# Weight remainders one item later on VectorE, and the last visit's down products tile by tile

## The reference

```python
x = layernorm(x + attention(x))            # 16 heads of 16 features
x = layernorm(x + recurrence(x, ctx))      # a scan over the tokens with exp(k), exp(-k)
x = layernorm(x + moe(x))

def moe(x):                                # E=8 experts, K=128 tokens for each: every token
    Sm = swapaxes(softmax(x @ Wg.T), 1, 2)
    G, I = top_k(Sm, K)
    ex = take_along_axis(x[:, None], I[..., None], axis=2)
    h1 = gelu(ex @ W1 + b1)                # 256 -> 1024
    out = G[..., None] * (h1 @ W2 + b2)    # 1024 -> 256
    return zeros_like(x).at[arange(b), I].add(out)
```

## Time and profile before

| | us |
|---|---|
| runs, median (lowest, highest) | 942.67 (942.16, 943.93) |
| the profiled execution, its time | 944.04 |
| its span | 942.3 |
| TensorE busy | 892.0 |
| VectorE busy | 599.3 |
| ScalarE busy | 579.7 |
| GpSimd busy | 79.2 |

### The profile page before, as it was taken

The page is one execution under the profiler, slowest core; times in us unless marked ns, Lnnn a source line. Parts: engine busy times, 40 slices in busy tenths (PEclk is TensorE's granted clock), DMA queues, the critical chain, the costliest instruction groups (busy, mean ns, idle before and its releaser), DMA issues.

```text
span 942.3 us, 17858 instructions
## 1 busy us (share of the span) xinstructions
PE 892.0 (95%) x6672; PEld 815.4 (87%) x6672; DVE 599.3 (64%) x1246; ACT 579.7 (62%) x991; POOL 79.2 (8%) x116
## 2 busy tenths in 40 slices
PE   4759888999999999999999999999999999999997
PEld 3659888889988988989998989889998999899997
DVE  5888879777656574665676564656756564433574
ACT  4438875786655666665566666655666665444684
POOL 2330012000110010200120001200110000000000
PEclk8669989999999999999999999999999999999999
DMA  7617999967755554555645454554545455555340
GB/s 226 211 48 247 363 349 314 316 211 247 234 179 151 172 163 144 165 169 156 187 127 177 159 183 153 151 175 156 173 131 184 148 173 167 191 192 164 114 137 12
DMA packets 144693, 172.43 MB, mean 183 GB/s; under 512 B 11208, under 2 KB 110816, under 8 KB 144608
## 3 DMA queue, kind: packets, MB, share of 16 engines
q1 hardware_dynamic: 144608, 171.29, 56.6%
HBM read 135.60 MB, written 35.65 MB: 182 GB/s over the span
## 4 chain that ended last, share of the span: by engine, by line
PE 85%; DVE 8%; ACT 4%; issue 1%; DMA 0%; POOL 0%; SPq 0%; POOLq 0%; ACTq 0%; DVEq 0%
PE down_ps L736 13%; PE down_ps L737 12%; PE down_ps L738 12%; PE up_ps L511 12%; PE up_ps L513 12%; PE up_ps L512 12%; PE bank L564 2%; PE bank L511 2%; PE bank L513 1%; PE bank L512 1%; PE bank L550 1%; PE bank L533 1%; DVE w_lo L893 1%; ACT h_all L836 1%; PE bank L582 1%
## 5 line engine op out<-in xcount | busy, mean ns | idle before, releaser
L836 ACT ACTIVATE h_all<-up_ps,b_all 128x512 f32<-128x512 f32 (+1 forms) x296 | 183.3, 635 | 256.7 <-PE up_ps L513 255.2
L893 DVE TENSOR_TENSOR h_lo<-h_all,h_hi 128x512 fp32r<-128x512 f32 x256 | 177.5, 693 | 221.3 <-ACT h_hi L827 220.8
L736 PE MATMUL down_ps<-w_hi,h_hi 128*128 128x256 f32 x1024 | 295.3, 288 | 2.9 <-DVE acc L1074 2.9
L737 PE MATMUL down_ps<-w_lo,h_hi 128*128 128x256 f32 x1024 | 289.9, 283 | 0.0
L738 PE MATMUL down_ps<-w_hi,h_lo 128*128 128x256 f32 x1024 | 289.6, 283 | 0.0
L511 PE MATMUL up_ps<-x2t_hi,w_hi 128*128 128x512 f32 (+1 forms) x592 | 222.5, 376 | 1.6 <-DVE x2t_lo L893 0.9
L513 PE MATMUL up_ps<-x2t_hi,w_lo 128*128 128x512 f32 (+1 forms) x592 | 217.1, 367 | 0.0
L512 PE MATMUL up_ps<-x2t_lo,w_hi 128*128 128x512 f32 (+1 forms) x592 | 216.3, 365 | 0.0
L736 PEld LDWEIGHTS down_ps<-w_hi,h_hi 128*128 128x128 f32 x1024 | 195.3, 191 | 11.6 <-issue 2.0
L737 PEld LDWEIGHTS down_ps<-w_lo,h_hi 128*128 128x128 f32 x1024 | 196.0, 191 | 6.8
L738 PEld LDWEIGHTS down_ps<-w_hi,h_lo 128*128 128x128 f32 x1024 | 195.8, 191 | 0.0
(11 more groups left out here) (193 smaller groups left out, 997.7 us busy)
## 6 DMA issues: line engine op xcount, KB each, us to landing
w_hi<-w_parts SPq DMA_DIRECT2D x200, 256.0 KB, 3.0
w_lo<-w_parts SPq DMA_DIRECT2D x200, 256.0 KB, 3.3
w_raw<-in_w_dram SPq DMA_DIRECT2D x96, 256.0 KB, 4.0
w_parts<-w_hi SPq DMA_DIRECT2D x64, 256.0 KB, 3.9
w_parts<-w_lo SPq DMA_DIRECT2D x64, 256.0 KB, 4.3
x_in<-in_x_dram SPq DMA_DIRECT2D x8, 256.0 KB, 3.8
ctx_sb<-in_ctx_dram SPq DMA_DIRECT2D x8, 256.0 KB, 3.9
out_dram<-acc SPq DMA_DIRECT2D x8, 256.0 KB, 2.5
```

The lines of the kernel that those rows point to most:

```text
L736: nc.tensor.matmul(ps, hi, w2h[:, c, :], start=c == 0 and j == 0, stop=False, skip_group_check=True)
L737: nc.tensor.matmul(ps, hi, w2l[:, c, :], start=False, stop=False, skip_group_check=True)
L836: a = nc.scalar.activation(h_all[:, unit % HALL, k * wide:(k + 1) * wide], up_ps[unit % 2][:, k * wide:(k + 1) * wide], ACT.Gelu_apprx_tan ...
L893: return nc.vector.tensor_tensor(dst, src, hi.bitcast(F32), ALU.subtract)
```

## The change

First, VectorE takes the remainder of a weight piece with the item behind the one on which ScalarE rounds it (`splits_before`). Within an item the remainder stays the last but one thing it does. ScalarE and SyncE keep their places in the line. Second, the four down steps of the last visit are replaced by `last_down(0)` and `last_down(1)`: the products of tile 0 for all four units, then those of tile 1, each tile in a bank of its own. Each tile then has its own sum, statistics, root, norm and store of 128 KB.

```diff
+    def splits_before(i):
+
+        return [piece for n in range(VISITS) for k in range(len(ITEMS[n])) if FIRST_ITEM[n] + k == i - 1 for piece in splits(n, k)]
...
-            store(NPAIR - 1)
-            sp.wait_ge(stored, 16 * NPAIR)
+            for t in range(PAIR):
+                sp.wait_ge(out_ready, NPAIR + t)
+                sp.dma_start(out[PAIR * (NPAIR - 1) + t], acc[:, (NPAIR - 1) % 2, t]).then_inc(stored, 16)
+            sp.wait_ge(stored, 16 * (NPAIR + 1))
...
+            def last_down(j):
+
+                n = VISITS - 1
+                free = [freed(n, 0), EVACUATED[n]][j]
+                pe.wait_ge(added, free)
+                for u in range(G):
+                    weights(n, 1, u)
+                    pe.wait_ge(h_ready, FIRST_UNIT[n] + u + 1)
+                    for k in range(2):
+                        c = 2 * u + k
+                        cols = slice(k * TOK + j * S, k * TOK + (j + 1) * S)
+                        ps = by_tile(down_ps[(down_banks(n)[0] + j) % 2])[:, j, :]
+                        slot = (FIRST_UNIT[n] + u) % HALF
+                        mm = product(ps, h_hi[:, slot, cols], h_lo[:, slot, cols], w2h[:, c, :], w2l[:, c, :], c == 0, c == FC - 1)
+                mm.then_inc(last_done, 1)
...
-                    else:
+                    elif visit < VISITS - 1:
                         down(visit, u)
...
+            for j in range(PAIR):
+                last_down(j)
...
+            def finish_last(t):
+
+                n, p = VISITS - 1, NPAIR - 1
+                tile = acc[:, p % 2, t]
+                dve.wait_ge(last_done, t + 1)
+                nc.vector.scalar_tensor_tensor(out=tile, in0=by_tile(down_ps[(down_banks(n)[0] + t) % 2])[:, t, :],
+                                               scalar=gate[:, p % 3, t, n % E:n % E + 1], in1=tile,
+                                               op0=ALU.mult, op1=ALU.add).then_inc(added, 1)
+                dve.wait_ge(added, EVACUATED[n] + t + 1)
+                nc.vector.bn_stats(stats[:, t, :], tile).then_inc(ln3_step, 1)
+                dve.wait_ge(ln3_step, 2 * (p + t) + 1)
+                nc.vector.tensor_copy(spare[:, 2:3], stats[:, t, 1:2])
+                nc.vector.bn_aggr(moments[:, 2, t, :], stats[:, t, :]).then_inc(ln3_step, 1)
+                dve.wait_ge(ln3_rstd, p + t + 1)
+                nc.vector.tensor_scalar(tile, tile, moments[:, 2, t, 0:1], rstd[:, 2, t:t + 1],
+                                        ALU.subtract, ALU.mult).then_inc(out_ready, 1)
...
-                    for visit, i, q in splits(n, k):
-                        split_lo(visit, i, q)
+                    for piece_before in splits_before(FIRST_ITEM[n] + k):
+                        split_lo(*piece_before)
...
-            add_expert(VISITS - 1)
-            finish(NPAIR - 1, 0)
-            finish(NPAIR - 1, 1)
+            for t in range(PAIR):
+                finish_last(t)
...
-            finish(NPAIR - 1)
+            for t in range(PAIR):
+                pool.wait_ge(ln3_step, 2 * (NPAIR - 1 + t) + 2)
+                nc.gpsimd.tensor_tensor(var_eps[:, 2, t:t + 1], moments[:, 2, t:t + 1, 1], eps_row[:, t:t + 1], ALU.add).then_inc(ln3_eps, 1)
+                pool.wait_ge(ln3_eps, NPAIR + t)
+                nc.gpsimd.tensor_tensor(rstd[:, 2, t:t + 1], var_eps[:, 2, t:t + 1], power[:, t:t + 1], ALU.pow).then_inc(ln3_rstd, 1)
```

More of the change, by code:

```diff
@@ L360, in decoder_layer @@
         down_done = sem("down_done")
+        last_done = sem("last_done")
         added = sem("added")
```

## The result

| | before | after |
|---|---|---|
| median of 20 runs each, us | 942.65 (941.75 to 945.57) | 945.48 (942.39 to 947.43) |
| mean of the same runs, us | 942.97 | 945.37 |
| profiled execution, us (span) | 944.04 (942.3) | 944.20 (942.4) |

The ratio after to before is 1.0025, with a 95% interval from 1.0017 to 1.0033: the changed kernel is slower by 0.25%, 2.4 us in the mean. The forecast was 943.6, a change of less than 0.2%; the measured time lies in its range (941.2 to 946.9), and near the 945.3 of rival A.

A forecast was written before the change was run, and what follows sets the result against it. TensorE, busy 892.0 us of 942.3, bounds the kernel; only its idle time, a lowered clock and the tail count. Late remainders +0.75 and last visit with tail +0.2 sum to +0.95 on the median 942.67: 943.6 us, range 941.2 to 946.9.

The forecast's parts named there:

- rival A: Clock falls in TensorE's new idle time: one fall +2.65 us, 945.3; two falls 947.0; chance 0.28.
- U(1,0): Item 4, at 77.77 us: TensorE waits for a later weight remainder and starts at about 78.8, +1.0 us carried through.
- 110.29 and 132.29: TensorE's waits ending at these times: as many remainders in each chain after as before, cost 0.
- SyncE's queue: Loads and keeps behind remainders: taken as 0, covered by backlog and late reading; otherwise at most 1.0 us once more.
- Items 29 to 36: Wait ending at 155.40 us: BACK's sum starts 0.4 earlier, wait goes from 2.07 to 1.65 us, -0.4.
- Items 41 to 43: Wait ending at 169.26 us: the expert's sum comes behind a remainder, idle 1.22 becomes 1.75 us, +0.5.
- Item 483: Wait ending at 897.10 us: item 482 loses its remainder, sums start earlier, TensorE's idle 0.35 us goes, -0.35.
- The last visit: Last 48 products: tile 0 needs the fourth unit after 18, TensorE stands from 932.1 to about 933.5, +1.4 us.
- The tail: After the last product: one tile's sum, statistics, aggregates and norm leave it, -1.2 us; power and store taken as 0.
- The lower end of the range, 941.2: Half of the faster rival: only the clock at 110.29 spared, and the store's gain; that rival's chance 0.10.

The follow-up runs named there:

- e11: Kernel before with only the remainders of items 2 to 29 one item later: 943.86 us, ratio 1.0009 (0.9998 to 1.0021).
- e2: Kernel before with only the last visit done tile by tile, remainders on time: 942.07 us, ratio 0.9996 (0.9987 to 1.0006).
- e10: Same kernel as e4, run once more: ratio 1.0032 (1.0020 to 1.0045) to the kernel before, mean +2.95 us.
- e1: Kernel before with all remainders one item later, last visit unchanged: 946.08 us, ratio 1.0032 (1.0020 to 1.0044).
- e5: Kernel before with last visit tile by tile and only the remainders of items 30 to 36 and 482 late: 940.14 us, ratio 0.9975.
- e4: Kernel before with only the remainders of items 0 and 1 one item later: 945.95 us, ratio 1.0030 (1.0019 to 1.0041).
- e8: e6 plus unread products in the idle times before 110 us (13) and 132 us (30): 939.12 us, ratio 0.9972.
- e12: e8 plus 15 unread products in the idle time before 155 us: 938.54 us, ratio 0.9953 to the kernel before.
- e6: e5 with ScalarE rounding the last W2 piece ahead of the last GELU: 939.76 us, ratio 0.9970 to the kernel before.
- e3: The changed kernel, but with the remainders of items 0 and 1 on time: 944.69 us, ratio 1.0011 to the kernel before.
- e7: e4 plus 8 unread products in U(1,0)'s wait, behind that for GELU: ratio 1.0022 to the kernel before, mean +1.68 us.
- e9: e4 plus 14 unread products ahead of all of U(1,0)'s waits: ratio 1.0021 to the kernel before, mean +1.84 us.

## Why the prediction failed where it did

The range held the time, and slower was the forecast's sign. Its size was not right: +0.95 us forecast, +2.8 measured between the medians and +2.4 between the means, where a change under 0.2% had the chance 0.62 and rival A 0.28. By its steps:

- **U(1,0), +1.0: right.** Idle 1.78 for 1.75, for w_lo, carried through to 110 in full.
- **110.29 and 132.29, 0, and SyncE's queue, 0: the second failed.** The wait at 110 is unchanged (1.80), as counted. But "a piece is read seven items after its split" named the wrong reader: the one that is near is ScalarE's next rounding into the same buffer, which waits for the keep. I had it as "if that cover were gone", at most 1.0. The cover is gone from 111 to 125 us, where the DMA share is over 1.0 (it is so in the kernel before too, without a wait), and e11 shows the chain: 1.47 of waits, 1.18 more idle time at 132 than e2. In the trace of after the stretch from 110 to 132 is 0.6 longer than before once the fall of the clock in the latter (1.5: 22.00 against 20.46 in e10) is taken off; in e1 it is 1.6 longer, of which 0.7 comes back by 155.
- **Items 29 to 36, -0.4: right in sign, wrong in place.** The wait before 155 did not go from 2.07 to 1.65; it is 2.04. What vanished is a wait of 0.46 for the turned x at 149, and from 132 to 155 it takes 21.83 instead of 23.11. This contains what 132 gives back. Over 110 to 155 it is 0.6 less than before, the fall of the clock again taken off; in e1, 0.9 more. e5, where items 2 to 29 are on time, shows the term by itself: 0.8 less than e2.
- **Items 41 to 43, +0.5: right** (1.73 for 1.75; the stretch is 0.51 longer).
- **Item 483, -0.35: right.** In size it was 0.6: from 170 us to the last 48 products it takes 0.63 less. The row says 0.35 because it counts from the modelled end of the product before. From start to start it is 0.63 (896.47 to 897.10) where the pitch is 0.12, and the first product behind the wait takes 0.1 longer; VectorE's sums were to start 0.60 earlier, and TensorE got all of it.
- **The last visit, +1.4: right** (7.34 for 5.94). The idle time in the row is only 1.14, since it counts from the modelled end of the product before, 0.28 after its start, where the pitch is 0.12, and the first product behind a wait takes 0.1 longer. Of it 0.44 belongs to the first edit, not 0.6: with the second edit alone (e2) it is 6.90.
- **The tail, -1.2: under-sized, -1.71.** The chain gained 1.25, of which 0.14 is the power (0.55 for one column, where I had 0.69 unchanged). The other 0.46 is the store, which I took at 0 gained. My row was the median over the eight stores of the kernel, 2.5, most of which share the queues with other transfers; the last one lands alone, in 2.1 before, and with half its size in 1.7. The Trainium skill (DMA: Bandwidth & Descriptors, the anatomy of one DMA) gives its figures for transfers issued by GpSimd, and these are issued by SyncE. By them the difference would be 0.3 (an estimate), and the trace shows 0.4; but they would make 2.3 and 2.6 us of the two sizes, where 1.7 and 2.1 were measured, so the agreement with the 2.5 of my row was an accident of that row.
- **The lower end of the range, 941.2,** doesn't follow from its terms: the clock spared (1.7) and the store's gain (0.3), off 942.67 or off 943.6, give 940.7 or 941.6. It played no part.
- **The clock, left to rival A at 0.28, and so put at nothing in the sum.** The low clock of after is 53.0 us in the mean, some 3 more than before's: 0.7 to 1.6 us by the two prices above. With the forecast's own sum of 0.95 this makes 1.7 to 2.5; measured 2.4. This agreement is partly luck. The terms as the trace of after shows them add up to nothing (1.00 - 0.65 + 0.51 - 0.63 + 1.40 - 1.71 = -0.08), not to 0.95, and the clock alone does not make 2.4. In e1's trace the first edit by itself costs 1.9 with the clock taken off (1.0 + 0.9 + 0.5 - 0.5), where the trace of after has 0.2 for it (its first four terms); the difference lies between 110 and 155 us, with the keeps. So of the 2.4 us the 1.0 of U(1,0) is shown; how the rest divides between the clock and the waits for keeps stays open. A single fall cost 1.5, not the 1.7 of rival A. My error on the clock was to treat the fall as belonging to one gap and as certain or absent. The rows I had, a gap of 1.81 with a fall and one of 2.07 without, already said that the length of the gap does not settle it (nor does any length in the later traces), and then a widened gap has its price as an expected value in the sum, not only as a rival. The Trainium skill (TensorE: Matmul & The Clock Gate, part 1) says the moments at which the chip decides run free of the kernel; the runs agree, in that e4 and e10 are the same kernel and the trace of e4 has a fall behind the gap at 110 and none behind that at 155, the trace of e10 the reverse.

## What to carry to other kernels

Before an instruction is moved later to "let others go first", list everything that its completion releases, the stores and the reuse of buffers among it, and look at the DMA share of that stage: with the queues full, a store issued later can come back as a wait of the engine that rewrites the buffer. Count for each chain what stands in front of its end before and after; moving all instances of an operation changes only a few chains, and it pays to move only those that gain (e5, 0.25% faster, against 0.25% slower for all, both with the second edit). Where the clock falls behind TensorE's gaps, here of 1.8 to 4 us, judge by the mean over many executions; and e8 and e12 suggest that one should fill all the gaps of a stretch or none.

## What the runs showed of the hardware

- A fall of the clock can be moved. Filling the gaps at 110 and 132 with products that nobody reads brought a fall at 150 (e8); only with the third gap filled was the clock at 1.00 from 76 us to TensorE's last product, and the kernel 0.47% faster than before (0.35 to 0.58) with 58 products more; without them it was 0.30% faster (e6). These falls are read from one trace of each.
- A gap of the same length, 1.80 to 1.84 before 110, had a fall behind it in the trace of before and in that of e4, and none in those of after, e1, e2, e3, e5, e6, e7, e9, e10 and e11.
- A microsecond at half the clock cost 0.24 us in the regression, which takes in the falls ahead of 76 us and behind the last product, in a kernel where TensorE is busy 95% of the time. One fall of 3.4 us cost 1.5 behind the gaps at 110, 132, 150 and 155 (22.00 for 20.46, 21.63 for 20.17, 15.35 for 13.87, 15.37 for 13.86), nearly the half. Doubling the fall behind 132 from 3.4 to 6.8 us added 0.9 to 1.1 (23.11 in before and e9, 22.05 and 22.23 in e10 and e2), where the half would be 1.7; I take it that VectorE's chain sets the time in its second part.
- With nothing else in the queues a store of 128 KB landed in 1.7 us and one of 256 KB in 2.1.
